# Narrow layers: the last 64 probability columns of two neighbouring units, laid side by side and transposed together

## What is computed

```python
# layers 0 and 2
logits = einsum('bhqd,bhkd->bhqk', q, k) * scale + col_bias
out = einsum('bhqk,bhkd->bhqd', softmax(logits), v) @ Wo + bo + residual
# layers 1 and 3
q = (rmsnorm(x, norm_w) @ wq).reshape(B, T, 16, 32)     # 4 query heads share one k, v head
attn = softmax(einsum('btgrd,bsgd->bgrts', qg, k) * scale)
x = residual + einsum('bgrts,bsgd->btgrd', attn, v) @ wo
```

## Time and profile before

| | |
|---|---|
| median of three runs | 2081.07 us (2079.6 to 2081.34) |
| span of the profiled execution | 2080.3 us |
| TensorE (PE) busy | 2042.1 us, 98% |
| VectorE (DVE) | 1389.7 us, 67% |
| ScalarE (ACT) | 966.4 us, 46% |
| GpSimd (POOL) | 644.7 us, 31% |
| mean granted TensorE clock | 0.997 |

### The profile page before, as it was taken

The page is one execution under the profiler, slowest core; times in us unless marked ns, Lnnn a source line. Parts: engine busy times, 40 slices in busy tenths (PEclk is TensorE's granted clock), DMA queues, the critical chain, the costliest instruction groups (busy, mean ns, idle before and its releaser), DMA issues.

```text
span 2080.3 us, 31294 instructions
## 1 busy us (share of the span) xinstructions
PE 2042.1 (98%) x11546; PEld 1764.4 (85%) x11546; DVE 1389.7 (67%) x2408; ACT 966.4 (46%) x1814; POOL 644.7 (31%) x519
## 2 busy tenths in 40 slices
PE   8999999999999998999999999999999989999998
PEld 8999988888888887788888888888888877888887
DVE  5322365775577557788888676557755775888886
ACT  3222354544355344555555454335443553555553
POOL 1000043311232244454443341223112533444441
PEclk9999999999999999999999999999999999999999
DMA  7889742222122222343333332212221232333332
GB/s 190 174 178 206 189 96 67 67 65 78 51 72 69 71 70 78 86 105 98 90 94 94 104 97 64 75 56 67 65 78 51 72 90 66 80 87 89 86 72 83
DMA packets 262537, 191.02 MB, mean 92 GB/s; under 512 B 197522, under 2 KB 199986, under 8 KB 259826
## 3 DMA queue, kind: packets, MB, share of 16 engines
q1 hardware_dynamic: 262386, 189.03, 35.6%
HBM read 132.66 MB, written 56.26 MB: 91 GB/s over the span
## 4 chain that ended last, share of the span: by engine, by line
PE 89%; DVE 6%; DMA 1%; ACT 1%; issue 1%; SPq 1%; POOL 0%; DVEq 0%; ACTq 0%; POOLq 0%
PE acc_bank L878 11%; PE acc_bank L261 8%; PE acc_bank L263 8%; PE acc_bank L262 8%; PE q_bank L836 8%; PE q_bank L840 8%; PE q_bank L838 8%; PE t_bank L858 7%; PE ctx_bank L261 3%; PE ctx_bank L262 3%; PE ctx_bank L263 3%; PE s_bank L799 2%; PE s_bank L261 2%; PE s_bank L796 2%; PE s_bank L802 2%; PE s_bank L263 2%
## 5 line engine op out<-in xcount | busy, mean ns | idle before, releaser
L1313 POOL TENSOR_TENSOR prob<-prob,rinv 128x1232 f32<-128x1232 f32 x128 | 288.5, 2254 | 1026.2 <-DVE rinv L1197 1026.2
L1055 ACT ACTIVATE q_s<-q_bank 128x512 fp32r<-128x512 f32 x192 | 115.0, 599 | 499.1 <-PE q_bank L840 494.8
L878 PE MATMUL acc_bank<-pT_s,vals_s 128*128 128x512 f32 x1024 | 337.8, 415 | 0.0
L1155 DVE TENSOR_REDUCE mx<-s_bank 128x4 f32<-128x308 f32 x512 | 240.2, 469 | 122.1 <-PE s_bank L263 63.2
L836 PE MATMUL q_bank<-x_s,w_s 128*128 128x512 f32 x768 | 318.9, 415 | 0.0
L840 PE MATMUL q_bank<-x_s,w_s 128*128 128x512 f32 x768 | 313.4, 408 | 0.0
L838 PE MATMUL q_bank<-x_s,w_s 128*128 128x512 f32 x768 | 312.8, 407 | 0.0
L261 PE MATMUL acc_bank<-o_s,w_s 128*128 128x512 f32 x752 | 303.6, 404 | 1.6 <-DVE o_s L1188 1.6
L263 PE MATMUL acc_bank<-o_s,w_s 128*128 128x512 f32 x752 | 296.7, 395 | 0.0
L262 PE MATMUL acc_bank<-o_s,w_s 128*128 128x512 f32 x752 | 296.7, 395 | 0.0
L1159 DVE TENSOR_TENSOR prob<-s_bank,mx 128x308 f32<-128x308 f32 x512 | 245.1, 479 | 27.4 <-DVE mx L1155 1.4
(11 more groups left out here) (107 smaller groups left out, 4095.5 us busy)
## 6 DMA issues: line engine op xcount, KB each, us to landing
stream<-x_back SPq DMA_DIRECT2D x128, 256.0 KB, 2.6
x_front<-stream SPq DMA_DIRECT2D x96, 256.0 KB, 3.3
x_back<-stream SPq DMA_DIRECT2D x96, 256.0 KB, 3.7
kvw_raw<-kvw SPq DMA_DIRECT2D x17, 1024.0 KB, 8.3
k_scr<-k_out SPq DMA_DIRECT2D x36, 308.0 KB, 10.4
keys_s<-k_scr SPq DMA_DIRECT2D x128, 77.0 KB, 2.5
v_scr<-v_out SPq DMA_DIRECT2D x8, 1024.0 KB
vals_s<-v_scr SPq DMA_DIRECT2D x512, 6.5 KB
```

Of the source, the lines that this page charges most:

```text
L878: mm = pe.matmul(out, w, pT_s[:, part], start=i == mine[0] and part == 2 * n and w is v[0], stop=i == mine[-1] and w is terms[-1][0] and p ...
L1155: dve.tensor_reduce(top, scored, AX_X, ALU.max).then_inc(s_max, 1)
L1313: pool.tensor_tensor(view, view, rinv[:, slot].unsqueeze(2).broadcast_to([P, TILES * GH, CTX]), ALU.mult).then_inc(p_norm, 1)
```

## The change

In a narrow layer an even unit's third block is no longer transposed in its own step. GpSimd copies the last 64 columns of each narrow unit into one half of the buffer `rest` (even units left, odd units right), and the full 128 columns are transposed in the odd unit's step; one transpose of 128 rows serves both units.

So the turns of an even unit are blocks 0 and 1, those of an odd unit 0, `TWICE`, 1, and the turns are now numbered by a list (`plan.t`). ScalarE and VectorE split the joint block in two halves of 64 rows. The last two products of an even unit's pv wait for the joint block: in the even step, pv stays open, the projection is run, and the two products come after it. Therefore `Plan.acc` places the first projection of such a step ahead of pv. The even unit's `split_o` and `rest_o` move to the start of the next step: on VectorE behind the four `tile_scores` and the late `add_result`. GpSimd's copy waits for the last reader of `rest`; VectorE's first subtraction for a unit waits for the copy of the unit two before it, whose place in `prob` it overwrites.

```diff
-            if self.ahead(s):
-                acc += projections
+            first = len(projections) if self.ahead(s) else 1 if self.split_values(s - 2) else 0
+            acc += projections[:first]
             if 0 <= s - 2 < NU:
                 acc += [("pv", s - 2, m) for m in range(kind(s - 2).Q)]
-            if not self.ahead(s):
-                acc += projections
+            acc += projections[first:]
+            turns += [(s - 1, n) for n in self.turns(s - 1)]
...
+    def split_values(self, u):
+        return 0 <= u < NU and kind(u).name == "B" and u % 2 == 0
+    def turns(self, u):
+        if not 0 <= u < NU:
+            return ()
+        return (0, 1, TWICE) if kind(u).name == "A" else (0, TWICE, 1) if u % 2 else (0, 1)
...  # TensorE, narrow step
                     run(v, 3)
                     turned(0)
                     run(q, half)
-                    run(v, 9)
-                    turned(1)
+                    run(v, 3 if behind else 9)
+                    late_turns = plan.turns(s - 1)[1:]
+                    turned(late_turns[0])
                     if plan.stats_at(s) is not None:
                         stats(plan.stats_at(s))
-                    turned(2)
-                    if not plan.ahead(s):
-                        for gb, m in plan.projections(s):
-                            project(gb, m)
+                    for n in late_turns[1:]:
+                        turned(n)
+                    if behind:
+                        projected(projections[:1])
+                        run(v, 2)
+                        projected(projections[1:])
+                    else:
+                        projected(projections)
                 elif s == NU:
-                    run(v, 9)
-                    for gb, m in plan.projections(s):
-                        project(gb, m)
-                    turned(0)
-                    turned(1)
-                    turned(2)
+                    run(v, 6)
+                    for n in plan.turns(s - 1):
+                        turned(n)
+                    projected(projections)
+                    run(v, 2)
                     finish((0, 1))
...  # VectorE, narrow step
                     for gb, m in plan.late(s - 1):
                         add_result(gb, m)
+                    if plan.split_values(s - 3):
+                        rest_o(s - 3, 0)
...  # VectorE, tile_scores
                 if t == 0 and u >= 2:
-                    dve.wait_ge(t_mm, 3 * (u - 2) + 3)
+                    dve.wait_ge(t_mm, plan.prob_read(u - 2))
+                    dve.wait_ge(p_gathered, u - 1)
...  # GpSimd, normalise
+                pool.wait_ge(p_norm, u + 1)
+                if u:
+                    pool.wait_ge(t_mm, plan.rest_read_before(u))
...
+                else:
+                    pool.tensor_copy(rest[:, :, 64 * slot:64 * slot + 64], prob[:, slot, :, SC - REST_B:SC])\
+                        .then_inc(p_gathered, 1)
```

More of the change, by code:

```diff
@@ L714, in load_vals @@
                     col = w * h % P
+                    if kind(u).name == "B" and blk == TWICE and u % 2:
+                        row = (row + 64) % P
                     sp.dma_start(vals[row:row + t1 - t0, blk, 0:last - first, col:col + w], src)\
@@ L845, in turn @@
             def turn(u, n):
+                item = plan.t[(u, n)]
                 if n == 0:
                     pe.wait_ge(p_norm, u + 1)
[L848 to L851, removed]
+                after(pe, t_lo, item - 1)
+                if n == TWICE:
+                    pe.wait_ge(p_gathered, u + 1)
                 for t in range(TILES):
[L853 to L858, removed]
+                    base = PAIR * n if kind(u).name == "A" else P * n
+                    p = rest[:, t] if n == TWICE else prob[:, u % 2, t, base:base + P]
+                    mm = pe.transpose(t_bank[item % 2][:, t * P:t * P + P], p, ident[:, :])
                 mm.then_inc(t_mm, 1)
@@ L949, in turned, with projected @@
                 def turned(n):
-                    if 0 <= s - 1 < NU:
+                    if n in plan.turns(s - 1):
                         turn(s - 1, n)
+                def projected(now):
+                    for gb, m in now:
+                        project(gb, m)
+                projections = plan.projections(s)
+                behind = plan.split_values(s - 2)
                 if a and s < 2:
@@ L964, in _ @@
                     turned(0)
-                    beside(scores(s, 3), v, 4)
-                    turned(1)
-                    turned(2)
-                    for gb, m in plan.projections(s):
-                        project(gb, m)
+                    beside(scores(s, 3), v, 2 if behind else 4)
+                    for n in plan.turns(s - 1)[1:]:
+                        turned(n)
[5 more added lines that the diff above has]
+                        projected(projections)
                     if plan.stats_at(s) is not None:
@@ L1067, in split_t @@
                     return
-                rows = 64 if n == TWICE else P
-                act.activation(pT_s[0:rows, 2 * n], t_bank[(3 * u + n) % 2][0:rows, :], ACT.Copy).then_inc(t_hi, 1)
+                act.activation(pT_s[:, 2 * n], t_bank[item % 2][:, :], ACT.Copy).then_inc(t_hi, 1)
             def split_o(u, m):
@@ L1123, in _ @@
                         split_o(s - 2, pv - 1)
-                    turned(1)
+                    for n in late_turns[:1]:
+                        turned(n)
                     bias(s + 1, 1)
@@ L1142, in _ @@
                         split_o(s - 2, m)
-                    turned(1)
-                    turned(2)
+                    for n in late_turns:
+                        turned(n)
                     fresh_x()
@@ L1221, in _ @@
                 q = rest_q(s + 1) if s + 1 < NU else iter(())
-                pv = kind(s - 2).Q if 0 <= s - 2 < NU else 0
+                pv = kind(s - 2).Q if 0 <= s - 2 < NU and not plan.split_values(s - 2) else 0
+                late_turns = plan.turns(s - 1)[1:]
                 def turned(n):
-                    if 0 <= s - 1 < NU:
+                    if n in plan.turns(s - 1):
                         rest_t(s - 1, n)
@@ L1248, in _ @@
                     if s >= 1 and not plan.rest_later(s - 1):
-                        rest_t(s - 1, TWICE)
+                        for n in late_turns[1:]:
+                            turned(n)
                     for gb, m in plan.projections(s):
```

67 lines of the change are left out of this document (39 added, 28 removed).

## The result

The changed kernel takes 2242.4 us (median; 2241.0 to 2247.2), the kernel before 2080.9 in the same comparison: a ratio of 1.078, with a 95% interval of 1.0765 to 1.0795. It is 161.6 us slower; 152 were forecast, and 2242 lies inside the range. (1.8 us of the time lie outside the span, in both kernels, where less than 1 had been taken; the difference is not touched by it.)

What follows compares the result with a forecast made beforehand. TensorE, busy for 98% of the span, was taken as the bound in narrow steps. The terms, -12 + 121 + 39 + 3 + 1 = 152 us, added to the median of 2081.07, gave 2233 us, range 2185 to 2266.

Steps and rivals of the forecast that it cites:

- transposes: TensorE, narrow steps: four transposes fewer per pair of units, 0.44 us each in 28 pairs, 12 us won.
- pv's wait: TensorE, 52 narrow steps: pv's first product waits for VectorE's late addition, 2.32 us each, 121 us lost.
- half clock: TensorE behind pv's waits: clock at 0.50 after half of them, 26 times 1.5 us, 39 us lost; bounds 0 and 78.
- steps without a late projection: Steps 34, 36, 98, 100: TensorE waits for the joint block's splits, 3 us lost; bounds 0 and 10.
- step 128: Step 128: pv waits for the last late addition with nothing between, 1 us lost.
- copies, moved loads: GpSimd's 64 copies and SyncE's later value loads: hidden, costed at nothing; uncovered, 26 us and some 4 us a pair.
- What is late next: nothing: Even steps: joint block's low part ready some half a microsecond before the projection ends, so held products do not wait.
- Rival 1: TensorE: the wait comes as worked out, but the clock stays at full; 2194 us, chance 0.18.
- rival 2: TensorE: the clock falls behind nearly every wait; 2272 us, chance 0.08.
- Rival 4: SyncE: its held queue becomes a second wait, 104 us on top, 2337 us; chance 0.06.
- Rival 3: pv's bank is emptied earlier, so only the transposes count; 2072 us, winning below a 0.23 us lag; chance 0.08.

Runs made afterwards that it cites:

- e8: e7 with one query product instead of three ahead of pv's first three; 2074.4 us, ratio 0.9971.
- e2: Kernel before, with only the two accumulator banks of pv and projection swapped in narrow even steps with a projection; 2233.4 us, ratio 1.0735.
- e1: Changed kernel, with VectorE's late addition put behind two of a narrow step's four tiles instead of all four; 2099.4 us, ratio 1.0091.
- e3: Changed kernel, with 16 extra block 0 transposes that nobody reads filling TensorE's wait ahead of pv; 2200.6 us, ratio 1.0584.
- e5: e1, with the two held products of narrow steps without a projection (34, 36, 98, 100) moved into the next step; 2093.5 us, ratio 1.0061.
- e6: Kernel before, with GpSimd's 64 copies and both their waits added, and nothing that reads the result; 2081.8 us, ratio 1.0007.
- e4: Changed kernel, with the second six query products put ahead of pv's first three in narrow steps but 34 and 98; 2176.3 us, ratio 1.0465.
- e7: e5, with three query products ahead of pv in late-addition steps and ScalarE splitting block 0 before the last exponential; 2080.6 us, ratio 0.9998.

## Why the prediction was right, and where it was not

| term | forecast, us | measured, us | from |
|---|---|---|---|
| transposes | -12 | -12 | 10.52 + 2.33 - 12.44 = 0.41 for a pair, 28 pairs; e8 |
| pv's wait | 121 | 121 | 52 x (2.26 + 0.07); e2, e1 |
| half clock | 39 | 41 | 25 stretches x 1.6, and 1.3 in step 127; e3 |
| steps without a late projection | 3 | 11 | steps 34 to 37 and 98 to 101; e5 |
| step 128 | 1 | 1 | one wait of 0.83 |
| copies, moved loads | 0 | 0 to 1 | e6; no wait of TensorE on them |
| sum | 152 | 162 | 161.6 between the medians |

**The wait** is the step on which all depended, and it held: both in its place (the two parities alike, 52 steps) and in its size. Even and odd steps came out at 12.8 and 12.4 us, where 12.9 and 12.4 had been worked out. e2 shows that the re-ordered list does it by itself, and e1 that VectorE's place for the addition is the other half of the cause. The forecast's split was a little off: the wait proper is longer than the lag taken (2.26 instead of 2.16), and less of the restart shows (0.07 instead of 0.16), because the 0.10 us between the addition's end and pv's start lies inside the first.

**What is late next: nothing.** True for the changed kernel, and by about the margin given: 0.4 us between the joint block's low part (974.62) and the products held back (975.01), where half a microsecond was forecast. But the margin was so thin that e1, e4 and e7 each used it up. A cover that is measured for one order holds for that order alone.

**The clock** held in the mean: half was taken, and 26 of 52 it was. That it came out exactly is luck: it was taken from four stretches, and e2, with waits of the same length, had 20 of 52. Rival 1 is out, since the clock fell to 0.975; rival 2 is out as well. The Trainium skill, "TensorE: Matmul & The Clock Gate", section "HAM oscillation — how this bites in real kernels", looks for the drop behind idle gaps longer than any of these, and by it the result would have been some 2201 (an estimate, 2242 - 41). The changed kernel's windows behind 2.09 us, and the 42 us between it and e3, decide against it here. Which of the waits bring the half clock is not explained: stretches of 2.06 to 2.09 us stand on both sides, in steps with the same order of work (42 and 44). The fixed turn of two steps with it and two without says that it is not chance from step to step; what decides, no run here shows.

**The step that failed** is "steps without a late projection", where 3 us were taken and 10 given as the bound; it was 11. I had seen that TensorE would wait for four splits there, and discounted it because VectorE was already late in the step that follows. Two things were missed. In steps 34 and 98 VectorE itself stood idle for 1.04 us ahead of the joint block's low part, until ScalarE had split the high part (the row at 841.93): the chain through two engines was longer than either one's lateness. In steps 36 and 100 VectorE was busy up to that row (864.03), and TensorE waited longer still. And behind these waits of 2.27 and 2.94 us came the half clock, which the forecast had priced for the 52 and not for these four: in e3, where only step 100 has it, the same eight steps lose 6.7 us instead of 11.2. e5, which takes this wait out of e1 and little else, gives back 6 of the 8 us that e1 loses here.

**The copies and the moved loads** were rightly costed at nothing, the copies by e6. Rival 4 saw no sign: no wait of TensorE for a load appears among its waits. The loads were not moved by themselves. Rival 3 named the right point, the lag between pv's start and the addition's end, but the bound given with it, a win for any lag below 0.23 us, did not hold: e1's is 0.04 (the addition ends 3.21 us into the step, pv stood at 3.17) and e1 is 18.7 us slower than the kernel before, and e7's is below zero and e7 gains nothing. The held products' wait and the steps without a late projection stood beside it. Only e8, with neither wait, wins.

## What to carry to other kernels

Where two kinds of work share alternating buffers by their number in a list, putting two of them in another order changes who waits for whom far from the place of the edit: for each item ask who used its bank last, and where the emptying of that bank stands in its own engine's queue. A wait on the engine that sets the time can cost more than its length, here a third again through the clock (41 on 121 us), so price both. And before work is moved to fill a hole, see what it was covering: e4 lost 47 of the 113 us that it was to win, most of them to that, and e7 its whole gain.

## What the runs showed of the hardware

Idle stretches of one length came out on both sides: of 52, all but three of them between 2.06 and 2.10 us, 26 had the half clock behind them and 26 had not, in a fixed turn of two steps with it and two without. With TensorE kept at work in the same stretches (e3) none had it, and the mean clock was 0.996. Nor had any of the 50 waits of at most 0.72 us that e4 leaves there; e4's mean of 0.992 comes from stretches in other steps and from the one wait of 1.75 us, in step 127.

A wait can also hide in the view that sums waits by releaser. 108.5 us stood there under "issue", with the addition ended 0.10 us before pv began; at a distance of 0.05 us the view had named VectorE. That the distance makes the difference is not shown. The timeline's row just ahead told what the name did not.
